# Layer-1 attention with one run of 64-column products a head, and the order of its helpers moved with it

## The reference, cut to what matters

```
q, k, v = (heads(xn @ w) for w in (Wq, Wk, Wv))
att = einsum('bhid,bhjd->bhij', q, k) / 8 + alibi       # alibi: -slope(head) * |i - j|
p = softmax(att, axis=-1)
out = einsum('bhij,bhjd->bhid', p, v).transpose(0, 2, 1, 3).reshape(B, S, INNER) @ Wo
```

## Time and profile before

| what | value |
|---|---|
| median of the runs | 2315.65 us |
| profiled execution | 2305.89 us, span 2304.0 us |
| TensorE busy | 2197.2 us, 95% |
| VectorE busy | 1829.4 us, 79% |
| POOL busy | 1385.3 us, 60% |
| ScalarE busy | 1234.0 us, 54% |
| granted clock, mean | 0.985 of full |

### The profile page before, as it was taken

One profiled execution on the slowest core, in us unless ns is written; L12 is line 12 of the kernel. 1 busy time (PEld: TensorE's weight loads), 2 busy tenths in 40 slices (PEclk: granted clock), 3 DMA queues, 4 the chain that ended last, 5 costly groups with the idle time before them and its releaser, 6 DMA issues. The chain is left out here.

```text
span 2304.0 us, 40435 instructions
## 1 busy us (share of the span) xinstructions
PE 2197.2 (95%) x10494; PEld 1381.0 (60%) x10531; DVE 1829.4 (79%) x4804; ACT 1234.0 (54%) x1664; POOL 1385.3 (60%) x751
## 2 busy tenths in 40 slices
PE   7989998899999999999999999999999999989995
PEld 4656665456565565656556565655556564449884
DVE  7788886788888888888888888888888887765555
ACT  2232323466666566666656666666666664444442
POOL 2112120578787787878778787887878787643331
PEclk9999999999999999999999999999999999999997
DMA  7050202000000100000100000010000000311114
GB/s 241 22 197 1 85 8 96 21 19 14 16 13 16 35 16 14 13 18 17 34 13 13 21 14 16 13 34 17 14 16 13 20 9 8 148 46 48 46 45 135
DMA packets 90230, 91.25 MB, mean 40 GB/s; under 512 B 22212, under 2 KB 74948, under 8 KB 90120
## 3 DMA queue, kind: packets, MB, share of 16 engines
q1 hardware_dynamic: 85800, 81.35, 11.4%
q0 software_dynamic: 4352, 8.99, 1.2%
HBM read 57.37 MB, written 36.33 MB: 41 GB/s over the span
## 5 line engine op out<-in xcount | busy, mean ns | idle before, releaser
L1624 ACT ACTIVATE big<-P 128x1024 f32<-128x1024 f32 x512 | 512.1, 1020 | 109.2 <-PE P L1993 85.5
L2007 PE MATMUL P<-big,V 128*64 128x512 f32 x2048 | 468.8, 599 | 1.0 <-ACT big L1630 1.0
L649 POOL TENSOR_TENSOR spair<-spair,big 128x1024 f32<-128x1024 f32 x192 | 457.4, 2382 | 15.9 <-DVE hp L810 1.3
L649 POOL TENSOR_TENSOR opair<-opair,big 128x1024 f32<-128x1024 f32 x192 | 457.3, 2382 | 15.0
L1031 DVE CUSTOM_DVE_ANT_0 big<-P,near 128x512 f32<-128x512 f32 x512 | 348.8, 681 | 112.2 <-PE P L1977 108.4
L1977 PE MATMUL P<-kq 96*128 96x512 f32 x1008 | 415.5, 433 | 14.2 <-DVE kq L1015 11.1
L1992 PE MATMUL P<-kq 97*128 97x512 f32 x1024 | 411.4, 402 | 5.7 <-issue 2.8
L1034 DVE TENSOR_REDUCE mhalf<-P 128x1 f32<-128x512 f32 x512 | 349.2, 682 | 79.0 <-PE P L1977 68.5
L1993 PE MATMUL P<-kq 128*128 128x512 f32 x1024 | 408.9, 399 | 0.0
L1977 PEld LDWEIGHTS P<-kq 96*128 96x128 f32 x1008 | 181.8, 190 | 214.3 <-issue 114.0
L2007 PEld LDWEIGHTS P<-big,V 128*64 128x64 f32 x2048 | 135.2, 136 | 265.0 <-issue 262.7
(11 more groups left out here) (316 smaller groups left out, 3663.1 us busy)
## 6 DMA issues: line engine op xcount, KB each, us to landing
slots<-later SPq DMA_DIRECT2D x4, 4224.0 KB, 15.5
kq<-auxrows SPq DMA_DIRECT2D x64, 128.0 KB, 2.3
big<-in_wex SPq DMA_DIRECT2D x8, 768.0 KB, 11.4
xt<-slots SPq DMA_DIRECT2D x76, 66.0 KB, 1.8
near<-in_aux SPq DMA_DIRECT2D x64, 64.0 KB, 1.8
big<-yrows SPq DMA_DIRECT2D x8, 512.0 KB, 7.2
wqk_hi<-wparts SPq DMA_DIRECT2D x62, 64.0 KB, 1.8
wqk_lo<-wparts SPq DMA_DIRECT2D x62, 64.0 KB, 1.9
```

Of the source, the lines that this page charges most:

```text
L649: pool.tensor_tensor(psum8[s][:, :], psum8[s][:, :], pfull[:, j % RING, :], ALU.add).then_inc(S["p_added"], 1)
L1624: act.activation(pfull[:, j, :], banks(2 * (j % 2)), ACT.Exp, scale=DH1 ** -0.5).then_inc(S["exp_done"], 1)
L2007: mm = pe.matmul(P[64 * i:64 * i + 64, 4, :], V1[:, j, s, :], half(pfull[:, j, :], i), start=(j == 0), stop=(j == T - 1))
```

## The change: its text

TensorE weighs all eight V tiles in one run after both halves of the projection and takes the sums of the same head right behind them. POOL scales the output of the head before after the seventh addition. VectorE moves all four inversions to its end, and takes low k of the first half ahead of low q. ScalarE rounds k before exponential 6 (with waits of its own), copies the sums at the head's start, the outputs after exponential 2, and writes the turned output between the first exponentials of the head after. The waits of bank 5 follow the new order. The core of the diff:

```diff
@@ POOL: add_head
-                    if behind and j == T - 2:
-                        scaled_out(1 - s, n - 1)
...
+                if behind:
+                    scaled_out(1 - s, n - 1)
@@ VectorE: head, from maxima (4, 1), (5, 0) on
-                if behind:
-                    invert(o, n - 1, 0)
+                bias(s, n, 6)
+                if ahead == 2:
+                    k_low(s, n + 2, 0)
                 maxima((5, 1), (6, 0))
-                bias(s, n, 6)
+                bias(s, n, 7)
                 maxima((6, 1))
                 if ahead == 2:
                     q_low(s, n + 2, 0)
-                    k_low(s, n + 2, 0)
-                bias(s, n, 7)
-                if behind:
-                    invert(o, n - 1, 1)
                 maxima((7, 0), (7, 1))
                 if ahead:
                     max_both(n + 1)
                     max_rows(n + 1)
+                if ahead == 2:
+                    q_low(s, n + 2, 1)
+                    k_low(s, n + 2, 1)
                 if behind:
-                    invert(o, n - 1, 2)
...
+                    for c in range(NINV):
+                        invert(o, n - 1, c)
@@ ScalarE: k_high, head
+                if not isinstance(n, int) or n > 1:
+                    act.wait_ge(S["st_mm"], T * (n - 2) + (i + 1) * TPH + ST_AT)
+                act.wait_ge(S["qk_mm"], 2 * n + i + 1)
...
+                if behind == 2:
+                    sums(o, n - 1)
                 exps(n, 0)
+                if behind == 2:
+                    turned_out(s, n - 2, p - 1, 0)
                 exps(n, 1)
+                if behind == 2:
+                    turned_out(s, n - 2, p - 1, 1)
...
                 exps(n, 5)
-                if behind:
-                    outputs(o, n - 1)
+                if ahead == 2:
+                    k_high(s, n + 2, 0)
+                exps(n, 6)
                 if ahead == 2:
                     q_high(s, n + 2, 0)
-                    k_high(s, n + 2, 0)
-                exps(n, 6)
@@ TensorE: head, from scores 5 on
                 maxima((4, 1))
-                if behind:
...
-                    sum_head(o, n - 1)
+                if s == 0 and ahead == 2:
+                    project_qk(s, n + 2, 0)
                 maxima((5, 0))
+                if s == 1 and ahead == 2:
+                    project_qk(s, n + 2, 0)
                 scores(s, n, 6)
-                maxima((5, 1))
-                if ahead == 2:
-                    project_qk(s, n + 2, 0)
-                maxima((6, 0))
+                maxima((5, 1), (6, 0))
                 scores(s, n, 7)
-                maxima((6, 1))
-                weigh(s, n, p, 0)
-                weigh(s, n, p, 1)
-                weigh(s, n, p, 2)
-                maxima((7, 0), (7, 1))
+                maxima((6, 1), (7, 0), (7, 1))
                 if ahead == 2:
                     project_qk(s, n + 2, 1)
-                weigh(s, n, p, 3)
...
+                for j in range(T):
+                    weigh(s, n, p, j)
+                if ahead == 2:
+                    pe.wait_ge(S["q_lo"], 2 * n + 6)
+                    pe.wait_ge(S["k_lo"], 2 * n + 6)
+                else:
+                    pe.wait_ge(S["v_in"], 2 * p + 2)
+                sum_head(s, n)
```

More of the change, by code:

```diff
@@ L717, in last_pairs @@
                 add_head(0, 2 * p)
-                add_head(1, 2 * p + 1, True, range(1, T - 2))
-                scaled_out(0, 2 * p)
+                add_head(1, 2 * p + 1)
                 pool.wait_ge(S["h_low_in"], at(16 * b + 16))
@@ L725, in last_pairs @@
                 pool.tensor_tensor(h_lo, h_lo.bitcast(F32), h_hi.bitcast(F32), ALU.subtract).then_inc(S["h_parts"], 1)
-                add_head(1, 2 * p + 1, False, range(T - 2, T))
                 pool.sem_inc(S["wo_ok"], 1)
@@ L741, in _ @@
             add_head(0, HEADS - 2)
-            add_head(1, HEADS - 1, True, range(1, 4))
+            add_head(1, HEADS - 1, False, range(1, 4))
             inverse_root("d0")
@@ L1069, in head @@
                 bias(s, n, 1)
-                maxima((1, 1))
+                maxima((1, 1), (2, 0))
+                bias(s, n, 2)
+                maxima((2, 1))
                 if out:
                     add_out(p - 1, 0)
-                maxima((2, 0))
-                bias(s, n, 2)
-                maxima((2, 1))
                 bias(s, n, 3)
@@ L1078, in head @@
                 bias(s, n, 4)
+                maxima((4, 0))
                 if out:
                     add_out(p - 1, 1)
-                maxima((4, 0))
                 bias(s, n, 5)
                 maxima((4, 1), (5, 0))
-                if behind:
-                    invert(o, n - 1, 0)
+                bias(s, n, 6)
+                if ahead == 2:
+                    k_low(s, n + 2, 0)
                 maxima((5, 1), (6, 0))
-                bias(s, n, 6)
+                bias(s, n, 7)
                 maxima((6, 1))
@@ L1639, in head @@
                 n, o = 2 * p + s, 1 - s
+                if behind == 2:
+                    sums(o, n - 1)
                 exps(n, 0)
+                if behind == 2:
+                    turned_out(s, n - 2, p - 1, 0)
                 exps(n, 1)
+                if behind == 2:
+                    turned_out(s, n - 2, p - 1, 1)
                 if s == 0:
                     values(p, 0)
-                if behind == 2:
-                    turned_out(s, n - 2, p - 1, 1)
                 exps(n, 2)
+                if behind:
+                    outputs(o, n - 1)
                 exps(n, 3)
@@ L1650, in head @@
                 exps(n, 4)
-                if behind:
+                if behind == 1:
                     sums(o, n - 1)
                 exps(n, 5)
-                if behind:
-                    outputs(o, n - 1)
+                if ahead == 2:
+                    k_high(s, n + 2, 0)
+                exps(n, 6)
                 if ahead == 2:
                     q_high(s, n + 2, 0)
-                    k_high(s, n + 2, 0)
-                exps(n, 6)
-                if ahead:
-                    k_again(o, n + 1)
                 exps(n, 7)
@@ L1665, in head @@
                     k_high(s, n + 2, 1)
+                if ahead:
+                    k_again(o, n + 1)
                 if ahead == 2:
                     q_again(s, n + 2)
-                if behind:
-                    turned_out(o, n - 1, p - 1 if s == 0 else p, 0)
             act.sem_inc(S["exp_done"], EXP_AT)
@@ L1766, in route_exp @@
                 act.activation(rexp[:, :, 0:E1], rlog[:, :, 0:E1], ACT.Exp).then_inc(S["rd_exp"], 1)
+            sums(0, HEADS - 2)
             exps(HEADS - 1, 0)
+            turned_out(1, HEADS - 3, ALL_PAIRS - 2, 0)
             exps(HEADS - 1, 1)
@@ L1772, in _ @@
                 exps(HEADS - 1, j)
-            sums(0, HEADS - 2)
+            outputs(0, HEADS - 2)
             exps(HEADS - 1, 5)
-            outputs(0, HEADS - 2)
             exps(HEADS - 1, 6)
@@ L1921, in project_v @@
                         pe.wait_ge(S["h_ok"], 2 * p + 2)
+                        pe.wait_ge(S["s_copied"], 2 * p)
                     pe.wait_ge(S["wv_in"], 32 * p + 32)
@@ L1935, in project_qk @@
                         pe.wait_ge(S["h_part_ok"], n)
[L1936 to L1939, removed]
+                        pe.wait_ge(S["v_in"], n)
+                    elif isinstance(n, int) and n == 3:
+                        pe.wait_ge(S["s_copied"], 1)
+                    else:
+                        pe.wait_ge(S["x_added"], n - 3 + X_AT)
                 else:
@@ L2043, in head @@
                     project_v(p, 0)
[L2044 to L2050, removed]
                 maxima((2, 0))
@@ L2053, in head @@
                 maxima((2, 1))
+                if out:
+                    pe.wait_ge(S["s_copied"], n)
+                    out_proj(p - 1, 0)
                 scores(s, n, 3)
                 maxima((3, 0))
-                if out:
-                    out_proj(p - 1, 1)
                 if s == 0:
@@ L2062, in head @@
                 maxima((4, 0))
+                if out:
+                    out_proj(p - 1, 1)
+                if behind == 1:
+                    pe.wait_ge(S["q_lo"], 2 * n + 4)
+                    pe.wait_ge(S["k_lo"], 2 * n + 4)
+                    sum_head(o, n - 1)
                 scores(s, n, 5)
                 maxima((4, 1))
[L2065 to L2072, removed]
-                    sum_head(o, n - 1)
+                if s == 0 and ahead == 2:
+                    project_qk(s, n + 2, 0)
                 maxima((5, 0))
+                if s == 1 and ahead == 2:
+                    project_qk(s, n + 2, 0)
                 scores(s, n, 6)
-                maxima((5, 1))
-                if ahead == 2:
-                    project_qk(s, n + 2, 0)
-                maxima((6, 0))
+                maxima((5, 1), (6, 0))
                 scores(s, n, 7)
-                maxima((6, 1))
```

(15 more changed lines are left out.)

3 lines of the change are left out of this document (removed).

## The result

The changed kernel takes 2382.41 us (median of four runs, 2378.13 to 2388.13) against 2315.43 for the kernel before on the same chip: a ratio of 1.029, with a 95% interval of 1.0264 to 1.0316. The forecast was 2375 us. The profiled execution took 2378.13 us, its span is 2376.3 us, and the mean granted clock is 0.987, as high as before (0.985).

The account below looks back on a forecast made before the run. TensorE's own queue was taken to bound layer-1 attention. A net +1.1 us a head over 61 heads, +67, less 8 at changes of batch, added 59 to the 2315.65 us median: 2375 us, range 2325 to 2435.

Parts of the forecast that it names:

- What it removes: On TensorE, two of three runs of 64-column products fall away at 0.33 us each: -0.65 us a head, -40 us in all.
- What it uncovers: TensorE stands ahead of the second projection for VectorE's low part of q: 1.75 us a head, net +1.1, +67 in all.
- The walk: Stepping both heads through at measured pitches: stands of 1.65 us in an odd head and 1.85 in an even one.
- rival (a): Smaller stand before the second projection: only the chain over ScalarE holds, 1.08 us a head, +18, 2334 us; chance 0.13.
- rival (d): No stand before the second projection, only the saved runs count: 2268 us; chance 0.07.
- TensorE's busy share of the stretch: Sign of a right forecast: TensorE's share of the layer-1 attention stretch falls from all of it to about 93%.
- The additions without a stop: POOL's unbroken additions hold VectorE's minima, about 3.1 us for 0.74 in every head; cost taken as nothing, cover gone.
- Rival (c): VectorE becomes the bound: each pair of minima waits for a whole addition, 4.9 us, giving 2448 us; chance 0.08.
- What moves off the path: POOL's seventh addition ends at 22.2 us, before TensorE reaches the sums at 23.4: no cost, cover 1.2 us.
- Changes of batch: At three changes of batch POOL's split work no longer delays the minima more than elsewhere: -8 us.
- The sum: The whole kernel: +67 - 8 on the profiled execution, carried to the median as 2315.65 + 59 = 2375 us.
- Rival (b), the clock: Stands make TensorE's clock fall to 1.2 GHz: 2430 us if in half of the heads, 2485 in all; chance 0.12.

Follow-up runs that it names:

- y3: x3 with two inversions earlier, the turned output later, and the kernel before's order from maximum (5,0) on, sums still behind V: 2295.45 us, ratio 0.9895.
- x1: The changed kernel with the four minima taken by a reduction over one operand instead of an operation on two: 2370.24 us, ratio 1.0228.
- x2: The changed kernel with three V tiles put back between the maxima (6,1) and (7,0): 2531.57 us, ratio 1.0934.
- x5: The kernel before with only POOL's additions without a stop, the scaling coming after the seventh: 2491.34 us, ratio 1.0757.
- x4: The kernel before with only the minima changed to read one operand: 2302.77 us, ratio 0.9936.
- x6: The kernel before with POOL's additions without a stop and the minima reading one operand: 2300.43 us, ratio 0.9938.
- x3: The changed kernel with three V tiles put back between the maxima and the minima reading one operand: 2323.76 us, ratio 1.0045.
- y1: x3 with two of the four inversions moved ahead of the maximum (7,0): 2310.45 us, ratio 0.9975.

## Why the prediction came out as it did

The direction, the place of the stand and the size were right; the time is 7 us over the 2375 forecast.

**What it removes** was right. The long run of 36 takes 7.88 us from 1025.99 to 1033.87, against 0.14 + 36 x 0.215 = 7.88. In y3 one run less makes an even head 0.30 us shorter; the step had 0.33 for it.

**What it uncovers** was right in place and in the mean over the two heads, and wrong in which head has which part. The walk gave a stand of 1.65 us for an odd head and 1.85 for an even one. The even head above stands 1.60. The odd head after it stands 1.47 ahead of the projection (1047.37 to 1049.78, less 0.94) and loses 0.38 more in its first half, chiefly 0.23 ahead of the scores of tile 2, which wait for exponential 0. That makes 1.85 for the odd head. The step had the wait for a bank in the even head, ahead of scores 5. So the mean, 1.73 us for 1.75, is in part luck: ahead of the projection the stand is 0.1 us shorter than the walk had it, and the wait in the odd head's first half, which it did not have, makes up for that. Net, between VectorE's transpositions of one head and the next (medians), the heads are 0.97 and 1.34 us longer (24.39 and 24.76 against 23.42), for a forecast of 1.1. VectorE's queue decides, as the walk had it, and not the chain over ScalarE alone: q is rounded from 1022.99 to 1023.58, and VectorE comes to its low part at 1024.36, 0.78 us later. With that rival (a) falls, and rival (d) with it. One of the step's signs did not come: TensorE's busy share of the stretch fell to 97.5% and not to about 93%, because short stands hide under the matmul before them. For the same reason the 235 busy us of the earlier trace rows don't show that TensorE never waited before: its weight loads waited 75.2 us for maxima.

**The additions without a stop**: the minima were forecast at 3.1 us and take 3.19, VectorE's end and the next first maximum at 25.2 and 25.3 us, and they are at 25.23 and 25.33 (1034.65 and 1034.75, from 1009.42). The cost of nothing is confirmed by x1 for ordinary heads, and that the cover is gone by x2, where the run is 12 products shorter. Rival (c), a pair of minima for each whole addition, did not come as a rule: 3.2 to 3.5 us in nearly all heads, not 4.9. But its picture of pairs is the right one. The first pair waits for the rest of an addition and the second for a whole one, so the sum depends on where in an addition the first minimum falls. In the median it is 2.85 us in x5, 3.25 in the changed kernel and 3.83 in x2, where the longest takes 5.06. The forecast 3.1 came from one row of a change of batch. The rule of the Trainium skill that the step weighed ("SBUF — State Buffer", section "Who interferes with whom") also says that a VectorE instruction with at most one SBUF input, outside its 2-port modes, does not contend with GpSimd. By that rule x1, x4 and x6 had to lose all holds; the runs agree, with a longest minimum of 166 to 169 ns where it was 2292.

**What moves off the path** held: POOL's seventh addition ends 22.3 us into the head (1031.70), the sums start at 23.5 (1032.91), for 22.2 and 23.4 forecast. The cover of 1.2 us is still there.

**Changes of batch** were put at -8 us. By the heads around the three changes it is about -8.5, but the agreement is luck. These heads were 15 us over the ordinary ones before, about twice what the step reckoned, and 6 us of that stay in the changed kernel, where the step left nothing over. x4 shows that held minima are the cause, since with one operand 13 of the 15 go, and x1 that the last 6 were held minima too.

**The sum** for the attention was +67 - 8 = +59, and the trace has +58.7. The medians have 67.0, 8 us more, and the cause of these 8 is open. From the last minima to the end of the span are 395.5 us in the profiled execution of before and 410.7 after; x4 and x6, which have the order of before there, have 411.1 and 405.6. So the profiled execution of before had a short end of its own, and no run ties the difference to the change.

**Rival (b), the clock,** fell in this kernel, and its mechanism is real: x5 shows it in 46 heads, at 1.2 to 1.5 us each. There the stand is one of 1.85 us; here it is 1.60 in pieces, the longest 0.6 (1023.66 to 1024.50, less 0.235), and the matmuls after it take 0.40 us. What decides stays open: x2 has more idle time a head than x5, in two pieces of 1.6 and 1.1 us on average, and the clock fell in 19 of its heads only.

## What to carry to other kernels

An instruction that looks misplaced in an engine's list may be cover: before two runs are joined to save their 0.33 us, list what the engine would issue in the gap and what chain on other engines runs meanwhile. Small VectorE instructions with two SBUF operands beside long POOL ones are worth rewriting with one operand: rewriting the same four instructions gave back 12, 13 or 191 us (x1, x4, x6), according to what stood behind them. And test causes together as well as alone, since here each fix by itself showed the wrong price for the other.

## What the runs showed that was not expected

- Four minima of 0.16 us each, held by back-to-back additions of POOL, made a kernel 191 us slower (x5 against x6), nearly three times what the whole change cost.
- A stand of 1.85 us once a head is followed by matmuls at the 1.2 GHz level in three heads of four (x5; 3.84 us of work in the head shown), so that in those heads it costs nearly double its length.
- A block of four reciprocals (3.39 us) at the end of VectorE's list is a stand of its own: it keeps VectorE from the next head's first maximum, so that TensorE stands 1.28 us when the block starts late (x2), and about 0.25 even when nothing is held (x3, y1).
